# Graph network on one core: VectorE makes all attention logits, edge rows are joined ahead, scatter groups are spread anew

## The reference

```python
# L0: three attention layers, 4 heads of 24
h = (x @ W).reshape(N, H, C)
e = leaky_relu(alpha_s[src] + alpha_d[dst], 0.2)
ex = exp(e - segment_max(e, dst)[dst])
x = relu(segment_sum(h[src] * (ex / (segment_sum(ex, dst)[dst] + 1e-16))[:, :, None], dst) + b)
# L1: sum over neighbours, then a two-layer MLP with batch norm
pooled = segment_sum(feature[src], dst) + (1.0 + eps[0]) * feature
# L2: dot-product attention over the edges, scores clipped to +-10
# L3: messages with edge features, then the same kind of MLP
msg = relu(x[src] + edge_attr @ We + be)
aggr = segment_sum(msg, dst)
```

## Time and profile before

| quantity | us |
|---|---|
| median of 3 runs | 5861.98 |
| lowest, highest | 5859.54, 5867.38 |
| profiled execution, its own time | 5863.81 |
| profiled execution, span | 5862.1 |
| `begin`: last count scatter issued | 1640.5 |
| first attention layer: first and last turned unit (L1281) | 1958.2, 2604.7 |
| second, third layer: last scatter of its groups | 3317.0, 4023.9 |
| node sum: first load, last instruction | 4060.2, 4207.8 |

### The profile page before, as it was taken

The page is one execution under the profiler, slowest core; times in us unless marked ns, Lnnn a source line. Parts: engine busy times, 40 slices in busy tenths (PEclk is TensorE's granted clock), DMA queues, the critical chain, the costliest instruction groups (busy, mean ns, idle before and its releaser), DMA issues. The chain is left out here.

```text
span 5862.1 us, 68109 instructions
## 1 busy us (share of the span) xinstructions
PE 3511.6 (60%) x25247; PEld 2219.0 (38%) x25248; DVE 3123.5 (53%) x3383; ACT 2625.6 (45%) x4143; POOL 3883.7 (66%) x3309
## 2 busy tenths in 40 slices
PE   3211222221034699988999889997868781667764
PEld 2211111111034455555555555554433330455542
DVE  3644555554369555445555455555579992333323
ACT  1000000000023689888888789894059891222211
POOL 1888888888884577666776578773020787777772
PEclk7555555555566899999999999998989995677765
DMA  8222222222279699757997479875542332332222
GB/s 296 20 18 20 20 18 10 1 1 0 9 251 361 169 195 199 161 115 150 195 193 156 103 164 201 184 153 152 178 166 79 109 130 74 110 81 74 75 53 24
DMA packets 427191, 683.75 MB, mean 117 GB/s; under 512 B 177678, under 2 KB 272397, under 8 KB 422768
## 3 DMA queue, kind: packets, MB, share of 16 engines
q0 software_dynamic: 236096, 287.22, 31.9%
q1 hardware_dynamic: 172432, 350.48, 17.8%
q10 hardware_dynamic: 18336, 41.70, 2.1%
HBM read 540.73 MB, written 138.43 MB: 116 GB/s over the span
## 5 line engine op out<-in xcount | busy, mean ns | idle before, releaser
L330 POOL DMA_INDIRECT counts<-plcell_add,plcell_slot x806 | 1253.9, 1556 | 385.4 <-issue 223.2
L1704 POOL DMA_INDIRECT emxg<-xtab,emsrc x856 | 944.0, 1103 | 448.4 <-issue 257.8
L714 ACT ACT_TABLE_LOAD x1 | 1.3, 1283 | 1613.2 <-PE mtps L702 1613.2
L377 PE MATMUL plpsR<-plpiece,plbefore 128*128 128x500 bf16 (+1 forms) x81 | 47.1, 582 | 813.8 <-DVE plranked L507 800.6
L422 DVE TENSOR_REDUCE plnlow<-plsame 128x13 f32<-128x1664 bf16 x62 | 117.0, 1888 | 661.6 <-DMA counts<-plcell_add,plcell_slot 661.5
L1788 PE MATMUL dotbanks<-emmsg,emsame 128*128 128x96 f32 x1712 | 316.3, 344 | 237.4 <-DVE emsame L1968 230.1
L1176 ACT ACTIVATE ga1prob<-ga1psE,ga1src_fifth 128x512 f32<-128x512 f32 (+1 forms) x700 | 407.2, 680 | 81.8 <-PE ga1psE L1281 79.1
L1176 ACT ACTIVATE ga2prob<-ga2psE,ga2src_fifth 128x512 f32<-128x512 f32 (+1 forms) x700 | 407.5, 683 | 77.0 <-PE ga2psE L1281 74.1
L1176 ACT ACTIVATE ga0prob<-ga0psE,ga0src_fifth 128x512 f32<-128x512 f32 (+1 forms) x700 | 407.1, 678 | 77.7 <-PE ga0psE L1281 74.7
L1788 PEld LDWEIGHTS dotbanks<-emmsg,emsame 128*128 128x128 f32 x1712 | 287.2, 250 | 382.2 <-issue 379.5
L1281 PE MATMUL ga0psE<-ident,ga0logit 128*128 128x128 f32 x2500 | 394.5, 288 | 55.8 <-DMA ga0logit<-log_counts 32.7
(11 more groups left out here) (403 smaller groups left out, 8577.9 us busy)
## 6 DMA issues: line engine op xcount, KB each, us to landing
ga0logit<-log_counts POOLq DMA_DIRECT2D x88, 512.0 KB
ga1logit<-log_counts POOLq DMA_DIRECT2D x88, 512.0 KB
ga2logit<-log_counts POOLq DMA_DIRECT2D x88, 512.0 KB
counts<-plzeros SPq DMA_DIRECT2D x32, 1250.0 KB, 32.7
mthalf<-counts SPq DMA_DIRECT2D x50, 800.0 KB
log_counts<-mtlogs SPq DMA_DIRECT2D x25, 1600.0 KB
ginhalf<-counts SPq DMA_DIRECT2D x50, 800.0 KB
dotlogs<-log_counts ACTq DMA_DIRECT2D x25, 1600.0 KB
```

The lines of the kernel that those rows point to most:

```text
L330: nc.gpsimd.indirect_dma_start(counts[w][:, :], bass.IndirectOffsetOnAxis(ap=cell_slot[:, g % 2, j:j + 1], axis=0), cell_add[:, g % 2, j:j ...
L377: nc.tensor.matmul(psR[:, f // RANK_BANK, 0:k * BINS], before[:], piece[:, n % 2, f:f + k, :].rearrange("p t b -> p (t b)"), start=True, s ...
L714: nc.scalar.activation(logs[:, n % OUTS, q, :], ps[:, u % 3, 0:BW], ACT.Ln, bias=tiny[:, 0:1], scale=math.e).then_inc(log_made, 1)
L1704: nc.gpsimd.indirect_dma_start(xg[:, h, t, :], None, xtab[:, :], bass.IndirectOffsetOnAxis(ap=src[:, g, t:t + 1], axis=0)).then_inc(gather ...
```

## The change

Four things change.

1. **Logits.** `add_bias` on ScalarE is gone. VectorE clamps the kept tiles too (`clamp_kept`, the same tensor_scalar with two column operands), and `finish_logit` becomes a plain tensor_tensor that adds the mask. ScalarE is left with exponentials and the copies of outputs in an attention layer. The order on VectorE is now: clamps of the added tiles, clamps of the kept tiles, the two adds, for run r + 2.
2. **Joined rows.** `begin` writes the edge rows (32 features and 2 ends) once to DRAM as `edge_rows`: SyncE loads features, ScalarE (idle there) copies features and ends together, SyncE stores. These 62 groups are paced by the count scatters, after the 54 transfers that clear `sorted_edges`. `edge_scatter` then loads one joined tile per group and all slots once, and GpSimd's copies go.
3. **Groups.** The layers get 16 groups each in place of 19, and `gin_pool` gets 9 (117 indirect DMAs).
4. **Spare cells.** The 128 spare cells of each count table are cleared by one 256-byte write ahead of the tables' own clearing, where before 128 writes of 2 bytes stood behind it.

```diff
-LAYER_GROUPS = ((5, 24), (24, 43), (43, 62))
+LAYER_GROUPS = ((5, 21), (21, 37), (37, 53))
+POOLING_GROUPS = (53, 62)
...
                 for part, done in zip(counts, zeroed):
+                    sp.dma_start(part[NP * NP:NP * NP + P, :].rearrange("(p f) o -> p (f o)", p=1), zeros[0:1, 0:P]).then_inc(done, 16)
+                for part, done in zip(counts, zeroed):
                     v = part[0:NP * NP, :].rearrange("(p j f) o -> j p (f o)", p=P, f=ZF)
                     for j in range(ZEROS):
                         sp.dma_start(v[j], zeros[:]).then_inc(done, 16)
-                    sp.dma_start(part[NP * NP:NP * NP + P, :], zeros[:, 0:1]).then_inc(done, 16)
...
+                def load_features(g):
+
+                    k = g % WHOLE_BUFS
+                    if g >= WHOLE_BUFS:
+                        sp.wait_ge(whole_made, 2 * (g - WHOLE_BUFS + 1))
+                    flat = feat[:, k, :, :].rearrange("p t k -> p (t k)")
+                    sp.dma_start(flat[0:P - 1, :], most[:, g * G * ED:(g + 1) * G * ED]).then_inc(feat_loaded[k], 16)
+                    n = min(G, EREST - g * G)
+                    if n > 0:
+                        sp.dma_start(flat[P - 1:P, 0:n * ED], rest[:, g * G * ED:(g * G + n) * ED]).then_inc(feat_loaded[k], 16)
+
+                sp.wait_ge(feat_cleared, 1)
+                load_features(0)
+                for g in range(NG):
+                    sp.wait_ge(added[1], 16 * (4 * SORTED_GROUPS + 2 * g + 1))
+                    if g + 1 < NG:
+                        load_features(g + 1)
+                    sp.wait_ge(whole_made, 2 * g + 2)
+                    sp.dma_start(edges["rows"][:, g * G:(g + 1) * G, :], whole[:, g % WHOLE_BUFS, :, :]).then_inc(whole_stored[g % WHOLE_BUFS], 16)
...
                 sp.wait_ge(slots_made, 1)
-                sp.dma_start(edges["ends"][:, :, :], ends[:]).then_inc(stored, 16)
                 sp.dma_start(edges["slot"][:, :], block_i[:]).then_inc(stored, 16)
-                sp.wait_ge(stored, 64)
+                sp.wait_ge(stored, 48)
+                for k in range(WHOLE_BUFS):
+                    sp.wait_ge(whole_stored[k], 16 * len(range(k, NG, WHOLE_BUFS)))
...
+                for g in range(NG):
+                    k = g % WHOLE_BUFS
+                    uses = range(k, g + 1, WHOLE_BUFS)
+                    act.wait_ge(feat_loaded[k], sum(32 if n * G < EREST else 16 for n in uses))
+                    if g >= WHOLE_BUFS:
+                        act.wait_ge(whole_stored[k], 16 * (g // WHOLE_BUFS))
+                    nc.scalar.activation(whole[:, k, :, 0:ED], feat[:, k, :, :], ACT.Copy).then_inc(whole_made, 1)
+                    nc.scalar.activation(whole[:, k, :, ED:RW], ends[:, g * G:(g + 1) * G, :], ACT.Copy).then_inc(whole_made, 1)
...
     return row_kept, len(chunks)
-def edge_scatter(nc, ctx, a, edges, tag, first, last):
-    sb = lambda n, s, d=f32: ctx.enter_context(nc.sbuf_tensor(tag + n, s, d))
-    sem = lambda n: nc.alloc_semaphore(tag + n)
-    STAGES = 2
+def edge_scatter(nc, ctx, edges, tag, first, last):
+    STAGES = 3
     count = last - first
-    LISTS = 4
-    slot = sb("slot", [P, LISTS, G], i32)
-    ends = sb("ends", [P, LISTS, G, 2])
-    feat = sb("feat", [P, STAGES, G, ED])
-    stage = sb("stage", [P, STAGES, G, RW])
-    feat_cleared, staged = (sem(n) for n in ("feat_cleared", "staged"))
-    list_loaded = [sem(f"list_loaded{k}") for k in range(LISTS)]
-    feat_loaded = [sem(f"feat_loaded{k}") for k in range(STAGES)]
-    scattered = [sem(f"scattered{k}") for k in range(STAGES)]
+    slot = ctx.enter_context(nc.sbuf_tensor(tag + "slot", [P, max(count, 1) * G], i32))
+    stage = ctx.enter_context(nc.sbuf_tensor(tag + "stage", [P, STAGES, G, RW], f32))
+    slots_loaded = nc.alloc_semaphore(tag + "slots_loaded")
+    rows_loaded = [nc.alloc_semaphore(f"{tag}rows_loaded{k}") for k in range(STAGES)]
+    scattered = [nc.alloc_semaphore(f"{tag}scattered{k}") for k in range(STAGES)]
     def steps(pool):
-        nc.gpsimd.memset(feat[:], 0.0).then_inc(feat_cleared, 1)
-        pool.wait_ge(feat_cleared, 1)
-        flat = a["edge_attr_32"].rearrange("e k -> (e k)")
-        most = flat[0:(P - 1) * ET * ED].rearrange("(p f) -> p f", f=ET * ED)
-        rest = flat[(P - 1) * ET * ED:E * ED].rearrange("(p f) -> p f", p=1)
-        loads = lambda i: 32 if (first + i) * G < EREST else 16
         def load(i):
-            g, k, m = first + i, i % STAGES, i % LISTS
-            pool.dma_start(slot[:, m, :], edges["slot"][:, g * G:(g + 1) * G]).then_inc(list_loaded[m], 16)
-            pool.dma_start(ends[:, m, :, :], edges["ends"][:, g * G:(g + 1) * G, :]).then_inc(list_loaded[m], 16)
-            rows = feat[:, k, :, :].rearrange("p t k -> p (t k)")
+            k, g = i % STAGES, first + i
             if i >= STAGES:
-                pool.wait_ge(staged, 2 * (i - STAGES + 1))
-            pool.dma_start(rows[0:P - 1, :], most[:, g * G * ED:(g + 1) * G * ED]).then_inc(feat_loaded[k], 16)
-            n = min(G, EREST - g * G)
-            if n > 0:
-                pool.dma_start(rows[P - 1:P, 0:n * ED], rest[:, g * G * ED:(g * G + n) * ED]).then_inc(feat_loaded[k], 16)
+                pool.wait_ge(scattered[k], 16 * G * (i // STAGES))
+            pool.dma_start(stage[:, k, :, :], edges["rows"][:, g * G:(g + 1) * G, :]).then_inc(rows_loaded[k], 16)
+        pool.dma_start(slot[:], edges["slot"][:, first * G:last * G]).then_inc(slots_loaded, 16)
         load(0)
+        pool.wait_ge(slots_loaded, 16)
         for i in range(count):
-            k, m = i % STAGES, i % LISTS
+            k = i % STAGES
             if i + 1 < count:
                 load(i + 1)
-            pool.wait_ge(feat_loaded[k], sum(loads(n) for n in range(k, i + 1, STAGES)))
-            pool.wait_ge(list_loaded[m], 32 * (i // LISTS + 1))
-            if i >= STAGES:
-                pool.wait_ge(scattered[k], 16 * G * (i // STAGES))
-            nc.gpsimd.tensor_copy(stage[:, k, :, 0:ED], feat[:, k, :, :]).then_inc(staged, 1)
-            nc.gpsimd.tensor_copy(stage[:, k, :, ED:RW], ends[:, m, :, :]).then_inc(staged, 1)
-            pool.wait_ge(staged, 2 * i + 2)
+            pool.wait_ge(rows_loaded[k], 16 * (i // STAGES + 1))
             for t in range(G):
-                nc.gpsimd.indirect_dma_start(edges["sorted"][:, :], bass.IndirectOffsetOnAxis(ap=slot[:, m, t:t + 1], axis=0),
+                nc.gpsimd.indirect_dma_start(edges["sorted"][:, :], bass.IndirectOffsetOnAxis(ap=slot[:, i * G + t:i * G + t + 1], axis=0),
                                              stage[:, k, t, :], None).then_inc(scattered[k], 16)
                 yield i * G + t
         for k in range(STAGES):
...
+                def clamp_kept(r, q):
 
                     j, c, h = runs[r]
                     first, width = RUN_FIRST[c] * P, RUN_TILES[c] * P
-                    dve.wait_ge(act_biased, act_count[r] + kept_tiles(j).index(q) + 1)
+                    if r >= L_BUFS:
+                        dve.wait_ge(turned, run_end(r - L_BUFS))
+                    nc.vector.tensor_scalar(logit[:, r % L_BUFS, q, 0:width], src_row[:, h, first:first + width], dst_bias[:, j % 2, q, h:h + 1],
+                                            low_bias[:, j % 2, q, h:h + 1], ALU.add, ALU.max).then_inc(kept_clamped, 1)
+
+                def finish_logit(r, q):
+
+                    j, c, h = runs[r]
+                    width = RUN_TILES[c] * P
+                    k, uses = mask_slot(r, q)
+                    dve.wait_ge(kept_clamped, kept_count[r] + kept_tiles(j).index(q) + 1)
+                    dve.wait_ge(mask_loaded[k], 16 * (uses + 1))
                     part = logit[:, r % L_BUFS, q, 0:width]
-                    nc.vector.scalar_tensor_tensor(part, src_row[:, h, first:first + width], least[:, block_first[j] + q, h:h + 1], part, ALU.max, ALU.add).then_inc(logit_ready, 1)
+                    nc.vector.tensor_tensor(part, part, mask[:, k, 0:width], ALU.add).then_inc(logit_ready, 1)
...
                     if ahead is not None:
                         for q in added_tiles(ahead):
                             clamp(r + AHEAD, q)
-                    for i in range(MOST + 1):
-                        if ahead is not None and i < len(kept_tiles(ahead)):
-                            finish_logit(r + AHEAD, kept_tiles(ahead)[i])
-                        if run == 2 and j and i == 1:
-                            output(j - 1)
+                        for q in kept_tiles(ahead):
+                            clamp_kept(r + AHEAD, q)
+                        for q in kept_tiles(ahead):
+                            finish_logit(r + AHEAD, q)
+                    if run == 2 and j:
+                        output(j - 1)
...
-                def add_bias(r, q):
-
-                    j, c, h = runs[r]
-                    width = RUN_TILES[c] * P
-                    k, uses = mask_slot(r, q)
-                    act.wait_ge(col_steps, COLS * (j + 1))
```

(10 more changed lines are left out.)

53 lines of the change are left out of this document (31 added, 22 removed).

## The result

The changed kernel took 6036.10 us (median of 5 runs, 6031.59 to 6041.99) beside 5861.98 (median of 5 runs of the kernel before). The ratio is 1.030, with a 95% interval of 1.028 to 1.031. The profiled execution has a span of 6034.8 us, 172.7 more than before.

The account below looks back on a forecast made before the run. In the layers ScalarE was taken to set the pace, with TensorE level in the tops. Layers gain 220, node sum costs 82, `begin` 8: 5862 - 220 + 82 + 8 = 5732 us, range 5630 to 5835.

Parts of the forecast that it names:

- `begin`, the step that failed: In `begin`, 124 added loads and stores slow the count scatters: 8 us longer, ends 0 and 44.
- Logits: Attention layers: blocks of 4 tiles fall from 99 to 89 us, of 3 from 83 to 72; layers gain 220.
- TensorE's own sum: 4-tile block of a layer: units 43, tops 6, values 30, output turn 2, sum 81 us.
- That they leave brings the layers little: Layers: moving nine groups to the node sum gains little, as GpSimd is not last there (82 us).
- GpSimd's sum of 82: 4-tile block of a layer: GpSimd's work and gaps 72 us, some 10 more for waiting on VectorE.
- Node sum: Node sum: 117 scatters, two per add, 70 left after the last add; 82 us longer, ends 17 and 105.
- DMA bounds the blocks: Rival, layers: DMA bounds 4-tile blocks at 93 us, layers gain 172, time 5780 (band 5770 to 5835); chance 0.19.
- Everything fits: Rival, layers: blocks of 82 and 67 us, layers gain 340, time 5612; chance 0.12.
- GpSimd is starved: Rival, layers: VectorE's six instructions in a row delay scatters and masks; layers gain 31, time 5921; chance 0.11.
- The bias was no bound: Rival, layers: TensorE at 92 of 99 us may be the pace already; gain 4 only, time 5948; chance 0.05.
- Scatters not held: Rival, node sum: scatters are hardly held, 17 us longer in place of 82, time 5667; chance 0.05.
- The shared port pair: Layers: if each GpSimd start waits half a VectorE instruction, GpSimd needs 93 to 95 us a block, 15 to 20 worse per layer.

Follow-up runs that it names:

- e1: The changed kernel with each 127-row feature load of `begin` issued as 112 rows and 15 rows: 5780.25 us, ratio 0.986 to the kernel before.

## Why the prediction was wrong, point by point

**`begin`, the step that failed.** "VectorE's one memset is early. What they can cost is DMA time under GpSimd's scatters": the mechanism was named, and then priced from the wrong row. The 44 clearing transfers of the earlier trace rows have 128 rows; the new loads have 127. By 0.08 us a transfer I had 10 us, 8 net, with 44 as the outer end; it was 254. With the loads cut as 112 and 15 the same traffic costs 19 where the sum had 10, and the spare cells give 17 back where it had 2: the net of 2 is near the forecast 8 because two errors cancel. All of the slowdown is this one line: without it the kernel is 1.4% faster than before. I had costed the transfers by bytes and count and never by their shape. The sign that the prediction names for being wrong here, count scatters whose gaps grow in the second half of `begin`, is the one that came.

**Logits.** The direction, the order of the bounds and the 3-tile blocks held: 72.4 us measured, 72 foretold; VectorE's tensor_tensor 1.21 for 1.1 to 1.3. The 4-tile blocks took 91 to 93 in the first layer and 91 to 97 in the others where I had 89. The term mis-sized is TensorE's own sum, 81 where the rows now give 87: the 0.23 us in each group of four, and the output turn. The layers gave 165 us, not 220, inside the 120 to 330.

**"That they leave brings the layers little" was wrong.** GpSimd's sum of 82 stood beside TensorE's 81, and I took the tie for slack. The 82 was also the sum for 16 groups, where the question was what 19 would cost: five more scatters in a 4-tile block, at 1.46 + 0.30 us, make it about 90. At 19 groups the new logits leave GpSimd last (77 of 82.6 us in a 3-tile block), and three groups fewer in a layer are worth 27 us a layer by the medians ((5774.43 - 5780.25 + 87) / 3). With the old logits they are worth 2. The 165 us are therefore not the logits' alone. By the layer stages, joined rows came first with 51, the logits at 19 groups added 35, the groups 67 to 87. That GpSimd's copies were worth nothing in the tables was right; in the layers the joined rows were worth those 51, which my sum counted only inside GpSimd's 82 (the copies and the fewer load issues were not tried apart).

**Node sum.** Two scatters per add, 71 left behind the last add (70 foretold), 86.4 us longer (82 foretold). This step was right in each part, and the move as such gains nothing: 81 us for 87.

**The rivals.** *DMA bounds the blocks*: no, by the stores from SyncE. *Everything fits*: no, TensorE's 87. *GpSimd is starved*: GpSimd's list does bound a layer, but at 19 groups and not at the 16 of the change. *The bias was no bound*: no; with the old logits three groups fewer in each layer gave 6 us, and at 16 groups the new logits were worth 115. *Scatters not held*: no. No rival put more than 44 us in `begin`, and that is why the range missed: with the loads well cut the sum of the parts as measured, 5862 - 165 + 86 + 2, is 5785, inside it. But 5785, like the 5780 of e1, is 50 us off the 5732 and lies in the band of the DMA case (5770 to 5835), whose mechanism the stores from SyncE speak against: a hit there would have been luck.

**The shared port pair.** In the node sum a scatter that starts in a two-input add is held until the add has ended, 3.81 us in place of 0.96. The Trainium skill ("SBUF — State Buffer", Who interferes with whom) says that VectorE with two inputs in SBUF holds the shared ports against GpSimd for the whole instruction, and the trace agrees. In the layers the mean scatter went from 1.25 to 1.36 us only, while VectorE was busy for 71 of 93 us in place of 55 of 99. The 93 to 95 us a block that the prediction gave GpSimd by half an instruction at each start did not come: with 16 groups it was busy for 67, and its gaps between scatters added 9.

## What to carry to other kernels

Before you price an added transfer by its bytes, look at how many rows it has and from which engine it is issued: 127 rows from SyncE took 11.1 us where 112 and 15 took 2.9, and GpSimd's scatters beside them landed in 5.7 us in place of 3.0. When two engines come out level in your sum, the one that you call hidden is the next bound, and the worth of a move has to be taken with the other edits in place: here the same nine groups were worth 6 us in the layers with the old logits and 81 with the new. Background work belongs in stages where its engine is idle and nobody waits at the end; a tail that stands alone costs its full length.

## What the runs showed of the hardware

- 206 KB loaded by SyncE as 127 rows: 11.1 us from issue to use; as 122 and 5 rows 7.05; as 112 and 15 rows 2.9. Scatters of 128 cells beside them landed in 5.7, 4.5 and 3.0 us, and in 3.0 without such loads.
- A single-row load issued behind the 127 rows kept SyncE for 3.13 us; behind the 112-row cut, for 0.25.
- Two stalls of TensorE of 2.2 us were followed by a granted clock of 0.50 (1.2 GHz), from 1.00 (2.4 GHz) before; over stretches of 7 us the two levels mix to 0.83 and 0.55. An output turn of 3.66 us took 6.87.
- A DMA share of 0.94 over a block did not mean that the engines were full: 624 more transfers of 128 rows and 48 of 221 KB cost 20 us in 1881, about what single profiles differ by. In short stretches the share reads 1.04 and 1.07, so it is not a true share of time.
